# Scaling and write-out of finished rows placed elsewhere in a fused two-block kernel on one core

## The reference

```python
h = _layernorm(x, axis=-1) * (1 + ca) + sa
x = x + ga * _L0_attn_ref(h, ...)          # two attentions, 16 heads of 8
h = _layernorm(x, axis=-1) * (1 + cb) + sb
x = x + gb * _L0_ffn_ref(h, ...)           # DEPTH = 2 layers
```

## Time and profile before

| | us |
|---|---|
| median of 3 runs | 1239.72 |
| the 3 runs | 2293.99, 1236.19, 1239.72 |
| profiled execution, its own time | 1240.99 |
| its span in the trace | 1239.1 |

### The profile page before, as it was taken

How to read it: one execution, slowest core, us unless ns; L and a number is a source line. 1 busy time by engine, 2 the same in 40 slices (tenths; PEclk the granted TensorE clock), 3 DMA queues, 4 the chain that set the end, 5 groups by cost and what they waited for, 6 DMA issues and landing times.

```text
span 1239.1 us, 37488 instructions
## 1 busy us (share of the span) xinstructions
PE 1120.7 (90%) x16048; PEld 696.0 (56%) x16048; DVE 957.8 (77%) x1524; ACT 822.6 (66%) x1207; POOL 381.4 (31%) x538
## 2 busy tenths in 40 slices
PE   4488889899889999688999999999999999999987
PEld 3133434344445667455666666666666666666654
DVE  7969693969668688886887788778878877877865
ACT  3498898989888876345655665665566566655644
POOL 1203220202200014665533433343333333323420
PEclk8599999999999999789999999999999999999999
DMA  3113130122113541110211111111111111110102
GB/s 109 34 23 127 50 107 20 34 86 103 34 67 103 171 153 54 52 26 20 75 28 23 28 28 23 28 28 24 23 24 24 27 24 27 27 24 19 33 10 69
DMA packets 41684, 61.71 MB, mean 50 GB/s; under 512 B 7440, under 2 KB 16816, under 8 KB 41520
## 3 DMA queue, kind: packets, MB, share of 16 engines
q1 hardware_dynamic: 39728, 58.44, 16.2%
q10 hardware_dynamic: 1792, 0.87, 0.3%
HBM read 22.61 MB, written 16.78 MB: 32 GB/s over the span
## 4 chain that ended last, share of the span: by engine, by line
PE 52%; DVE 3%; ACT 3%; issue 1%; DVEq 0%; ACTq 0%
PE psum L1392 9%; PE psum L1536 7%; PE psum L1481 6%; PE psum L1503 5%; PE psum L1467 4%; PE psum L1402 4%; PE psum L1412 4%; PE psum L1562 3%; PE psum L1489 2%; PE psum L1424 2%; PE psum L1452 2%; ACT ffn_probs L1770 2%; PE psum L1432 1%; PE psum L1458 1%; PE psum L1527 1%
## 5 line engine op out<-in xcount | busy, mean ns | idle before, releaser
L865 ACT ACTIVATE att_probs<-psum 128x1024 f32<-128x1024 f32 x352 | 334.9, 1028 | 39.3 <-PE psum L723 39.2
L1910 POOL TENSOR_TENSOR ffn_rot<-ffn_rot,ffn_rot_sin 128x512 f32<-128x512 f32 x128 | 160.1, 1272 | 378.5 <-DVE ffn_rot L1945 378.5
L764 PE MATMUL psum<-att_probs,att_v 128*32 128x256 f32 (+3 forms) x3072 | 178.6, 347 | 3.7 <-DVE att_probs L1058 3.1
L723 PE MATMUL psum<-att_q_stack,att_k_parts 64*128 64x512 bf16 (+2 forms) x1472 | 132.9, 273 | 43.2 <-ACT att_probs L865 32.1
L723 PEld LDWEIGHTS psum<-att_q_stack,att_k_parts 64*128 64x128 bf16 x1472 | 45.3, 94 | 143.5 <-ACT att_probs L865 105.3
L1763 ACT ACTIVATE ffn_max_t<-psum 68x128 bf16<-68x128 bf16 x64 | 17.5, 273 | 157.6 <-PE psum L1440 157.4
L764 PEld LDWEIGHTS psum<-att_probs,att_v 128*32 128x32 f32 x3072 | 79.8, 110 | 62.1 <-issue 37.7
L1058 DVE TENSOR_TENSOR att_probs<-att_probs,att_causal_mask 128x1024 f32<-128x1024 f32 (+1 forms) x80 | 94.7, 1199 | 25.7 <-ACT att_probs L865 25.5
L1770 ACT ACTIVATE ffn_probs<-psum 128x1024 f32<-128x1024 f32 x64 | 65.6, 1025 | 56.3 <-PE psum L1467 56.3
L1732 ACT ACTIVATE ffn_sq<-psum 128x512 f32<-128x512 f32 x128 | 74.6, 595 | 23.0 <-PE psum L1392 22.0
L1481 PEld LDWEIGHTS psum<-ffn_v_back,ffn_probs 128*64 128x64 f32 x1024 | 64.9, 138 | 31.9 <-ACT ffn_probs L1770 17.9
(11 more groups left out here) (237 smaller groups left out, 2396.4 us busy)
## 6 DMA issues: line engine op xcount, KB each, us to landing
ffn_v_back<-ffn_v SPq DMA_DIRECT2D x120, 130.0 KB, 2.4
att_q_stack<-q_rows SPq DMA_DIRECT2D x28, 512.0 KB, 3.7
q_rows<-att_q_high SPq DMA_DIRECT2D x21, 256.0 KB, 2.6
q_rows<-att_q_mid SPq DMA_DIRECT2D x21, 256.0 KB, 2.7
q_rows<-att_q_low SPq DMA_DIRECT2D x14, 256.0 KB, 4.1
xres<-in_hidden SPq DMA_DIRECT2D x4, 512.0 KB, 5.9
out<-ffn_qk_t SPq DMA_DIRECT2D x3, 512.0 KB, 3.3
tail_f_wqkv<-in_f_wqkv SPq DMA_DIRECT2D x1, 768.0 KB, 4.6
```

The lines of the kernel that those rows point to most:

```text
L723: ins = T.matmul(psum[:, banks[i] + at:banks[i] + at + width], k_parts[rows, p % 3, j, key:key + P], q_stack[rows, turn % 2, j, q0:q0 + wi ...
L764: ins = T.matmul(psum[32 * g:32 * g + V_PAD, (4 + cc) * BANK + lo - cc * BANK: (4 + cc) * BANK + hi - cc * BANK], v_of(p, kt, g, shift), p ...
L865: act.activation(probs[:, n % E_BUFS, 2 * j:2 * j + 2, 0:width], ps2((step % 2) * 2).rearrange("p (h c) -> p h c", h=2)[:, :, 0:width], AC ...
L1910: steps.did(pool.tensor_tensor(out, out, halves(k.rot_sin[:, n % 2, :])[:, :, 1 - half, :], ALU.add), g["added"] if half else None)
```

## The change

The change moves work and adds no arithmetic. On ACT the scaling of batch 0 goes from period 47 to 50, that of batch 1 from 55 to 58, and that of batch 2 is split: its first 64 partitions are scaled in period 63, and the others in period 64. The call now stands behind `head_roots` and, in period 64, behind `copy_hn`, instead of at the end of the period. Batch 0's write-out goes on PE into period 65, and on DVE behind the loop's last gate. Batches 1 and 2 go ahead of DVE's last three gates. Banks and waits are changed to suit.

```diff
--- before.py
+++ after.py
@@ -1282,7 +1282,7 @@
 EARLY_LOADS = 5
 TAIL_BATCH = {1: 3, 2: 4, 3: 5}
 GATES_AT = 6
-SCALE_AT = (47, 55, 63)
+SCALE_AT = {50: (0, 0, 2), 58: (1, 0, 2), 63: (2, 0, 1), 64: (2, 1, 2)}
 
 
 def ffn_stream(nc, psum, dram, keep, k, tail):
@@ -1313,9 +1313,9 @@
               3: tail.o_t[:, 3].rearrange("p (t d) -> p t d", t=TILES)}
     y = k.qk_t[:].rearrange("p i s -> p (i s)")[:, 0:B * S].rearrange("p (b t d) -> p b t d", b=B, t=TILES)
     OUT_PARTS = ((0, 0, TILES), (1, 0, TILES), (2, 0, TILES), (3, 0, TILES // 2), (3, TILES // 2, TILES))
-    OUT_BANKS = (4, 0, 2, 4)
+    OUT_BANKS = (2, 4, 2, 0)
     LAST_X_BANK, LAST_HN_BANK, LAST_Y_BANK = 0, 2, 6
-    LAST_UP_BANKS = {(0, 0): 3, (1, 0): 0, (2, 0): 1, (0, 1): 7, (1, 1): 4, (2, 1): 5}
+    LAST_UP_BANKS = {(0, 0): 7, (1, 0): 0, (2, 0): 1, (0, 1): 4, (1, 1): 5, (2, 1): 7}
     x_bank = lambda c: LAST_X_BANK if c == LAST else MLP_BANK
     hn_bank = lambda c: LAST_HN_BANK if c == LAST else MLP_BANK
     up_bank = lambda c, j, part: (LAST_UP_BANKS if c == LAST else UP_BANKS)[j, part]
@@ -1521,8 +1521,7 @@
             def xn_transposes(c):
                 pe.wait_ge(g["xn_ready"], c + 1)
                 if c == LAST:
-                    pe.wait_ge(g["maxed"], STREAM)
-                    pe.wait_ge(g["mt_copied"], STREAM)
+                    pe.wait_ge(g["out_gated"], 1)
                 for i in range(CHUNK_TILES):
                     ins = T.transpose(psum[:, hn_bank(c) * BANK + i * P:hn_bank(c) * BANK + (i + 1) * P],
                                       k.xn[:, i, :], keep.ident[:])
@@ -1600,10 +1599,11 @@
             def last_up(j, part):
                 if j == 0 and part == 0:
                     pe.wait_ge(g["hn_ready"], LAST + 1)
+                    pe.wait_ge(g["y_added"], LAST)
                 if j == 0 and part == 1:
-                    pe.wait_ge(g["y_added"], LAST)
-                if j == 1 and part == 1:
-                    pe.wait_ge(g["out_gated"], 1)
+                    pe.wait_ge(g["out_gated"], 2)
+                if j == 2 and part == 1:
+                    pe.wait_ge(g["gelu_ready"], ALL_BLOCKS * LAST + 1)
                 up(LAST, j, part, g["a_in_psum"] if part else g["g_in_psum"])
 
             def last_residual():
@@ -1634,10 +1634,13 @@
             def write_out(i):
                 b, t0, t1 = OUT_PARTS[i]
                 pe.wait_ge(g["scaled"], i + 1)
-                if i == 1:
+                if i == 0:
+                    pe.wait_ge(g["maxed"], STREAM)
+                    pe.wait_ge(g["mt_copied"], STREAM)
+                if i == 2:
+                    pe.wait_ge(g["hn_ready"], LAST + 1)
+                if i == 3:
                     pe.wait_ge(g["gelu_ready"], ALL_BLOCKS * (LAST + 1))
-                if i == 3:
-                    pe.wait_ge(g["u_ready"], ALL_BLOCKS * (LAST + 1))
                 for t in range(t0, t1):
                     for s in range(2):
                         half = slice(64 * s, 64 * (s + 1))
@@ -1672,6 +1675,8 @@
                     query_scores(n - 1)
                 if live(n - 3):
                     project_out(n - 3)
+                if n == STREAM + 1:
+                    write_out(0)
                 if step == 2 and live_chunk(c):
                     up_gelu(c, 0, n)
                 if step == 1 and live_chunk(c):
@@ -1710,12 +1715,13 @@
                 down(LAST - 1, j)
             last_residual()
             xn_transposes(LAST)
-            write_out(0)
-            for part in range(2):
-                for j in range(ALL_BLOCKS):
-                    last_up(j, part)
-            for i in range(1, 4):
-                write_out(i)
+            write_out(1)
+            for j in range(ALL_BLOCKS):
+                last_up(j, 0)
+            write_out(2)
+            for j in range(ALL_BLOCKS):
+                last_up(j, 1)
+            write_out(3)
             for j in range(ALL_BLOCKS):
                 last_down(j)
 
@@ -1818,10 +1824,10 @@
                                          ACT.Copy), g["gates_copied"])
                 steps.settle()
 
-            def scale_rows(i):
+            def scale_rows(i, first, last):
                 b, t0, t1 = OUT_PARTS[i]
                 act.wait_ge(g["y_added"], final_chunk(b, t1) + 1)
-                for rows, shift in ((slice(0, 64), 0), (slice(64, P), 1)):
+                for rows, shift in ((slice(0, 64), 0), (slice(64, P), 1))[first:last]:
                     x = keep.xs[rows, b, shift + t0 * P:shift + t1 * P]
                     steps.did(act.activation(x, x, ACT.Copy, scale=k.gate_cols[rows, b:b + 1]), g["scaled"] if shift else None)
 
@@ -1840,6 +1846,8 @@
                     copy_hn(c)
                 if live(n):
                     head_roots(n)
+                if n in SCALE_AT:
+                    scale_rows(*SCALE_AT[n])
                 if step == 3 and live_chunk(c):
                     for j in range(ALL_BLOCKS):
                         gelu(c, j)
@@ -1856,8 +1864,6 @@
                         tail_evacuate(b, 1)
                 if n == GATES_AT:
                     copy_gates()
-                if n in SCALE_AT:
-                    scale_rows(SCALE_AT.index(n))
                 if step == 1 and live_chunk(c):
                     row_roots(c)
 
@@ -1869,7 +1875,7 @@
             row_roots(LAST)
             act.preload_act_table_set(GELU_SET)
             copy_hn(LAST)
-            scale_rows(len(SCALE_AT))
+            scale_rows(3, 0, 2)
             for j in range(ALL_BLOCKS):
                 gelu(LAST, j)
 
```

## The result

The changed kernel takes 1229.73 us in the median of 5 runs (1228.2 to 1231.1), the kernel before 1239.57 us. The ratio of the runs is 0.9937, with a 95% interval of 0.9920 to 0.9954; it leaves out the slow run of the kernel before, 2293.99 us, so it is not the ratio of the two medians. The profiled execution has a span of 1229.0 us, where it was 1239.1 us. I had forecast 1230.5 us.

The account below looks back on a forecast made before the run. PE, busy 90% of the span, was held by waits for DVE, delayed by batch-wide scalings ahead of the row roots. Savings 4.1 + 3.7 + 0 + 1.4 = 9.2 us took 1239.72 to 1230.5 us, range 1226.5 to 1236.

Parts of the forecast that it names:

- Batches 0 and 1, 4.1 us: Periods 47 to 50, 55 to 58: moving the scalings behind the head roots shortens two chunk cycles, saving 2.06 and 2.07 us.
- The cover: ACT's wait of 5.93 us in period 50, behind the head roots, claimed to hide the moved scaling of 2.31 us.
- Batch 2, 3.7 us: Periods 63 and 64: splitting the scaling saves 2.15 us of PE's waiting and 1.60 us of lowered clock.
- PE even, 0: Write-out transposes on PE: 0.56 us more in period 65, 0.56 us less among the last up projections, sum 0.
- Output writes, 1.4 us: End of the span: the last output write lands 2.4 us after its issue in place of 3.8.
- The moved waits: Behind the loop: DVE's sum fits between gates, first up projection and down projection are not late; cost 0.
- B: PE's clock in period 64 saves nothing in the median, leaving 7.6 us saved, 1232.1 us; chance 0.14.
- C: The last output write still takes 3.8 us, a fixed cost of such writes: 1231.9 us; chance 0.08.
- D: The scaling does not fit its new places or did not hold DVE; half of 7.8 us returns, 1234.4; chance 0.08.
- E: PE's clock falls at the end of period 64 and stays down to the end: 1249.4 us, slower; chance 0.02.

Follow-up runs that it names:

- the write-outs alone: The changed kernel with the three scalings put back at the end of periods 47, 55 and 63; ratio 0.9993 to the kernel before.

## Why the prediction was right

The forecast of 9.2 us stands against 7.8 us by the ratio (5.7 to 9.9) and 8.6 us by the trace from period 46 on. That the median of 1230.5 us was met within 0.8 us is in part luck. I took the saving off a median of 1239.72 us, while in the later comparisons, of 11 to 22 runs each, the kernel before has medians of 1236.9 to 1237.5 us. The base was about 2 us too high and the saving 0.6 to 1.4 us too large, and the two errors offset each other. By its own steps:

- **Batches 0 and 1, 4.1 us.** Measured 4.02, and alone 4.0. The cover was there, and even period 47 had enough of it.
- **Batch 2, 3.7 us.** Measured 2.16 + 1.59 = 3.75, and 3.75 as the difference of two kernels. The two prices are separate: filling the pause with useless work gives the 1.6 us back and not the 2.15.
- **PE even, 0.** This is the term that was mis-sized: it is -0.84 + 0.16 = -0.68 us. The prediction named its own sign of this, period 65 longer by more than 0.6 us, and the sign came: 10.87 us became 11.71. I had priced a write-out transpose at the mean of a row of 40, 0.035 us, on both sides. In period 65 16 of them take 0.65 us, and with the up projection behind them it is 0.84 in place of 0.56. At the end, 40 in 1.40 us became 16 in 0.64 (the chain has records of 12) and 8 in 0.40, and the 12 up-projection passes, 5.42 us in one piece, became 2.83 + 2.77 = 5.60 us in two, so 0.16 us was saved and not 0.56. A block of 16 put into other work cost 0.3 us more than my price in the one place and 0.4 us in the other. The kernel before has such a block of its own, batch 0's write-out, with a wait for ACT behind it. Its row would have been the nearer price:

```profile
1223.16 0.72 PE L1645 MATMUL psum<-ident,xs 64*128 64x64 f32 x16
```

- **Output writes, 1.4 us.** Measured 1.52. Leaving out the writes in front gives 1.58. With 0.91 us of transfer, 2.3 us leave 1.4 us that are fixed. The Trainium skill, "DMA: Bandwidth & Descriptors", section "Anatomy of one DMA", gives about 2.0 us for the path by GpSimd, which is not this one; here the measurement decides.
- **The moved waits.** DVE's first sum fitted exactly, the first up projection was not later (5.55 us both times), and the down projection was not held by the gates.

Of the rivals, B (the clock saves nothing in the median) is refuted as far as the profiled executions go: the clock fell in all six with the pause of 3.31 us, and in none of the six with 1.17 us. Where it fell differed: by the granted clock of the stretches 0.1 us after the head transposes' start in the first profile of before, 1.0 us after it in the second, and 0.6 us ahead of it with the write-outs alone. That agrees with the Trainium skill, "TensorE: Matmul & The Clock Gate", section "What's actually happening", by which the monitor's window runs freely; a whole fall was never missing. C and D are refuted by the rows above. E did not happen, and in no profile did the clock stay down until the end. Its condition, a pause of 3.31 us, was too long: 2.00 us already brought the clock down.

The larger part of my range was the 3.5 us between two runs of one kernel. The two profiles of the kernel before differ by 4.0 us, and 3.9 of that lie ahead of period 46. They lie ahead of period 12 even, since all profiles agree from there to period 46. The granted clock goes with a part of it. Between 480 and 600 us it is 0.89 or 0.90 in four profiles and 0.91 to 0.93 in the other ten. The four take 136.2 to 136.9 us from the value copy of period 0 to that of period 12, the others 133.1 to 134.7. That the clock is the cause was not tested.

## What to carry to other kernels

Side work on an engine that is a third idle is free only where that engine's next instruction waits anyway; the same pair of instructions cost 2.0 us each time at the end of a period and nothing in the middle of it. When a wait moves TensorE's start, count the clock apart from the wait, since 2.00 us of pause cost 1.46 us more where 1.17 us cost nothing. And on the engine that ends the chain, look for its own pauses before cutting a full row of its work in two.

## What the runs showed of the hardware

- A pause of 2.00 us on TensorE, with one of 0.94 us about 1.6 us before it, took the granted clock to 0.50, at a price of 1.46 us; pauses of 1.69 us (periods 48 and 56) and of 1.17 us (with the same 0.94 us before it) did not. In the seven profiles with a fall it came between 0.6 us ahead of the head transposes' start (write-outs alone) and 1.4 us behind it (pause of 2.00 us).
- The price of a fall was 1.46 us after 2.00 us and 1.50 to 1.59 us after 3.31 us. It was 1.29 us after 3.31 us where the fall came 0.6 us ahead of the work.
- An output write of 256 KB lands 2.3 us after its issue with a free queue, one of 512 KB after 3.2 us; behind others it waits for their bytes, which move at 284 to 291 GB/s.
